# Output projection of three batches moved into the attention steps, with two rearrangements before the first step

## The chip, the cores and the metric

The kernel runs on one core of one Trainium2 chip. The time is device microseconds of one execution. The kernel before was run three times: 1149.98, 1150.86 and 1151.96 us, median 1150.86 us. One further execution was recorded by the profiler; all rows below are from that one.

## The reference, cut to what matters

```python
xn = _layernorm(x)                                   # x: (4, 2048, 256), 16 heads of 16
q, k, v = xn @ q_w, xn @ k_w, xn @ v_w               # each (4, 16, 2048, 16) after the reshape
scores = (q * sigmoid(unity_scale)) @ k.T / sqrt(16)
allowed = (j % 4 == 0) | (abs(i - j) <= 8)
attn = softmax(where(allowed, scores, -inf)) @ v
ffn  = float8_e4m3fn(clip(xn / input_scale, -448, 448)) * input_scale @ w_dq.T + bias
x + (attn @ o_w + o_b) + ffn                         # (4, 2048, 256)
```

## The kernel before, in words

The 8192 rows are 16 chunks of 512 rows (CH), four in each batch (CPB). There are two parts, one after the other on every engine.

**The projection part** (`part_project`) goes once over the 16 chunks, c = 0 to 15. For a chunk TensorE (PE) makes q (L551), the transposes of the next chunk (L561), k (L572), v (L582) and the fp8 linear product (L597, waits for `y8_ready`). ScalarE (ACT) writes the high halves of q and k as f16 (L327, L347) and copies v out of PSUM (L354); VectorE (DVE) writes the low halves (L435, L440) and adds the linear product to `base`, which holds x (L376); GpSimd (POOL) rounds to fp8 (L296, L299). SyncE (SP) stores q and k of a chunk in twelve DMAs of 128 KB (L262) and v in four of 256 KB (L256). There are two buffers for these halves, so ACT's L327 of chunk c waits until all twelve stores of chunk c-2 have landed (`qk_stored`).

**The attention part** (`part_attend`) has 64 steps: 16 groups of four heads (four groups a batch), each with four chunks of 512 queries. The steps are unrolled, and the order within a step is written out by hand in `tensor_attend.body`. A step has three strands:

- *Units.* Ten of them a step, for queries one and two steps ahead: PE makes scores with queries on partitions (L1092 far keys, L1103 and L1110 near keys), DVE reduces each to a maximum (L1002, L1005). Two units fit into PSUM. The maxima go through DVE L985, four small POOL instructions (L798 to L804), a PE transpose (`score_peaks`, L1048), an ACT copy (L927) and two DMAs by SP (`move_negmax`, L846) into rows of `q_op`, and the first scores of the next step wait for that.
- *Scores and weights.* PE makes scores with keys on partitions (L1057, L1067, L1070), ACT takes the exponential (L934, L939), PE multiplies with v (L1127, L1134). `SCORES` lists the order; the scores go round three PSUM banks, and PE may refill a bank when ACT is done with it (`s_used`).
- *The division.* ACT copies the result (L918), SP moves the sums (L838), DVE inverts them (L978), SP stores and broadcasts them (L870, L888), POOL multiplies (L789), SP stores the step's result to `attn_dram` (L892).

`Step(0, -2)` and `Step(0, -1)` hold the units and negated maxima that step 0 needs. Before them SP waits for all stores of the projection part and loads v (`load_v`, L823), and ACT waits for these stores too.

After the last step the output projection runs by itself: for each of the 16 chunks the transposed attention result is loaded (`load_heads`, L760, two DMAs of 256 KB: SP for the first batch, within the last steps, ACT for the others), PE multiplies it with `o_w` (L1207, and L1229 for the last chunk, in quarters), DVE adds it to `base` (L1018, L1029) and SP stores the chunk (L904, 512 KB; L907, 128 KB each).

## Time and profile before

| | |
|---|---|
| median of three runs | 1150.86 us |
| the profiled execution | 1153.22 us, of which the span 1151.4 us |
| busy, share of the span | PE 94%, DVE 82%, ACT 70%, POOL 22% |
| TensorE clock granted, mean | 0.976 of full speed |
| DMA, mean | 131 GB/s |
| projection part | 0 to about 237 us |
| steps 0 to 63 | 266 to 1084 us |
| output projection | 1084 to 1151 us |

"Busy" of PE is from a matmul's start to its modelled end. Matmuls overlap in the array, so a PE that is busy in the profile may still be between two starts with nothing to start; how far apart the starts are tells more. The span begins at the core's first instruction.

### The profile page before, as it was taken

The page shows a single profiled execution, that of the slowest core. Times are in us where ns is not written, and L with a number is a line of the kernel's source. Part 1 is how long each engine was busy: PE and PEld are TensorE (multiplying, and loading weights), DVE is VectorE, ACT ScalarE, POOL GpSimd, SP SyncE. Part 2 cuts the span into 40 slices and gives each one's busy share as a digit, 9 for nine tenths or more (in the row PEclk, how much of TensorE's full clock was granted, in tenths as well). Part 3 has the DMA queues.
Part 4 walks back from the last instruction along what each step waited for, and adds up shares of the span by engine and source line. Part 5 has one row for each costly group of instructions (what it writes and reads, how often), then busy time and mean ns, then how long its engine had stood idle before and what let it go on. Part 6 is the DMA issues. An engine that isn't in the chain of part 4 may idle for free.

```text
span 1151.4 us, 28768 instructions
## 1 busy us (share of the span) xinstructions
PE 1080.5 (94%) x10944; PEld 492.7 (43%) x10944; DVE 944.7 (82%) x1203; ACT 808.6 (70%) x1524; POOL 249.3 (22%) x381
## 2 busy tenths in 40 slices
PE   5899999947999999999999999999999999999896
PEld 3566666512333333333333334333333333333585
DVE  5888777475999999999999999999999999998132
ACT  2443444215888888888888888888888888888500
POOL 1433333210221222122121212212121212212100
PEclk9999999956999999999999999999999999999998
DMA  6677777662223333333333333333333333232367
GB/s 190 190 230 229 218 229 235 197 194 66 90 85 110 96 102 91 109 96 94 101 105 98 91 96 113 94 95 97 109 95 92 100 104 101 89 104 85 97 247 271
DMA packets 192506, 150.74 MB, mean 131 GB/s; under 512 B 35628, under 2 KB 171564, under 8 KB 192364
## 3 DMA queue, kind: packets, MB, share of 16 engines
q1 hardware_dynamic: 188424, 142.10, 40.4%
q10 hardware_dynamic: 3952, 6.88, 1.7%
q8 instruction: 85, 1.39, 0.5%
q14 instruction: 45, 0.37, 0.1%
HBM read 79.86 MB, written 67.77 MB: 128 GB/s over the span
## 4 chain that ended last, share of the span: by engine, by line
PE 66%; DVE 10%; SPq 8%; issue 7%; DMA 6%; ACT 1%; POOL 0%; ACTq 0%; DVEq 0%; POOLq 0%
PE ps_attend L1127 16%; PE ps_attend L1057 12%; PE ps_attend L1092 9%; DVE peak_far L1002 9%; PE ps_attend L1134 6%; SPq L262 5%; PE ps_attend L1067 4%; PE ps_attend L1103 3%; DMA heads<-attn_dram 3%; PE ps_attend L1070 3%; SPq L256 3%; PE ps_project L582 2%; PE ps_project L551 2%; PE ps_project L572 2%; PE ps_attend L1110 2%
## 5 line engine op out<-in xcount | busy, mean ns | idle before, releaser
L1002 DVE TENSOR_REDUCE peak_far<-ps_attend 128x2 f32<-128x1024 f32 x512 | 608.6, 1221 | 55.1 <-PE ps_attend L1092 51.5
L934 ACT ACTIVATE probs<-ps_attend 128x512 f32<-128x512 f32 x1024 | 539.1, 597 | 54.9 <-PE ps_attend L1057 51.8
L1127 PE MATMUL ps_attend<-probs,v_op 128*32 128x512 f32 x2048 | 273.4, 606 | 0.0
L1057 PE MATMUL ps_attend<-q_op,k_op 51*128 51x512 f16 x1024 | 259.5, 387 | 14.4 <-DMA q_op<-negmax_rows 10.7
L1092 PE MATMUL ps_attend<-k_op,q_op 48*128 48x512 f16 x1024 | 186.6, 389 | 17.1 <-DVE peak_far L1002 15.5
L1057 PEld LDWEIGHTS ps_attend<-q_op,k_op 51*128 51x128 f16 x1024 | 77.8, 93 | 209.3 <-ACT probs L934 135.6
L939 ACT ACTIVATE probs<-ps_attend 108x512 f32<-108x512 f32 x256 | 138.9, 594 | 37.3 <-PE ps_attend L1070 37.3
L798 POOL CAST negmax<-peak 128x16 bf16<-128x16 f32 x64 | 12.6, 197 | 638.0 <-DVE peak L985 638.0
L1005 DVE TENSOR_REDUCE peak_near<-ps_attend 128x8 f32<-128x864 f32 x128 | 131.0, 1023 | 11.3 <-PE ps_attend L1110 11.1
L789 POOL TENSOR_TENSOR out_rows<-out_rows,share_rows 128x512 f32<-128x512 f32 x64 | 81.3, 1270 | 48.6 <-DMA share_rows<-shares_dram 46.0
L1067 PEld LDWEIGHTS ps_attend<-mask_q,mask_k 48*108 48x108 bf16 x1024 | 59.9, 125 | 67.8 <-ACT probs L934 55.3
L1092 PEld LDWEIGHTS ps_attend<-k_op,q_op 48*128 48x128 f16 x1024 | 49.9, 94 | 88.7 <-DVE peak_far L1002 70.0
L1067 PE MATMUL ps_attend<-mask_q,mask_k 48*108 48x128 bf16 x1024 | 78.6, 227 | 0.8 <-ACT probs L934 0.8
L327 ACT ACTIVATE qk_parts<-ps_project,ranges 128x1024 f16<-128x1024 f32 x16 | 17.8, 1114 | 82.2 <-DMA k_dram<-qk_parts 38.4
L1070 PE MATMUL ps_attend<-q_op,k_op 51*108 51x128 f16 x1024 | 73.6, 217 | 0.0
L1134 PE MATMUL ps_attend<-probs,v_op 108*32 108x128 f32 x2048 | 69.2, 276 | 0.0
L1127 PEld LDWEIGHTS ps_attend<-probs,v_op 128*32 128x32 f32 x2048 | 40.4, 108 | 58.4 <-issue 58.3
L296 POOL TENSOR_TENSOR quant<-quant,power 128x1024 f32<-128x1024 f32 x16 | 37.7, 2356 | 119.5 <-DVE qk_parts L440 84.8
L1103 PE MATMUL ps_attend<-mask_k,mask_q 48*128 48x216 bf16 x512 | 58.9, 259 | 3.3 <-DVE peak_far L1002 1.6
L551 PE MATMUL ps_project<-xnT,wq 128*128 128x512 f32 x128 | 60.3, 616 | 1.2 <-ACT xnT L334 1.2
L1070 PEld LDWEIGHTS ps_attend<-q_op,k_op 51*108 51x108 f16 x1024 | 61.5, 126 | 0.0
L1134 PEld LDWEIGHTS ps_attend<-probs,v_op 108*32 108x32 f32 x2048 | 52.1, 109 | 15.7 <-issue 13.7
(80 smaller groups left out, 1043.2 us busy)
## 6 DMA issues: line engine op xcount, KB each, us to landing
v_dram<-v_sb SPq DMA_DIRECT2D x64, 256.0 KB, 4.1
share_rows<-shares_dram SPq DMA_DIRECT2D x64, 256.0 KB
attn_dram<-out_rows SPq DMA_DIRECT2D x64, 256.0 KB, 5.7
v_op<-v_dram SPq DMA_DIRECT2D x48, 288.0 KB
q_dram<-qk_parts SPq DMA_DIRECT2D x96, 128.0 KB
k_dram<-qk_parts SPq DMA_DIRECT2D x96, 128.0 KB
q_op<-q_dram SPq DMA_DIRECT2D x128, 96.0 KB, 2.4
k_op<-k_dram SPq DMA_DIRECT2D x64, 144.0 KB, 3.1
```

The source lines that it names most:

```text
L551: last = nc.tensor.matmul(ps_q[:, m], wq[:, i, m * P:(m + 1) * P], xnT[:, k, i], start=(i == 0), stop=(i == KC - 1))
L934: ins = nc.scalar.activation(probs[:, r, h], ps_s[st.bank(kind)], ACT.Exp, scale=undo)
L939: ins = nc.scalar.activation(probs[0:WIN, ROUNDS - 1, h], ps_s[st.bank(kind)][0:WIN], ACT.Exp, scale=undo)
L1002: ins = nc.vector.tensor_reduce(peak_far[:, :, p, tile], banks, AX_X, ALU.max)
L1005: ins = nc.vector.tensor_reduce(peak_near[:, :, tile:tile + 2].rearrange("q f t p -> q f (t p)"), banks[:, :, 0:2 * PAIRS * WIN].rearrange ...
L1057: nc.tensor.matmul(bank, k[half(f, KM), keys], q[half(f, KM), p], start=True, stop=True).then_inc(s_ready, 1)
L1067: nc.tensor.matmul(banks[f][0:WIN, cols], mask_k[half(f), at_mask:at_mask + WIN], mask_q[half(f), tile * P:(tile + 1) * P], start=True, st ...
L1070: ins = nc.tensor.matmul(banks[f][0:WIN, cols], k[half(f, KM), at:at + WIN], q[half(f, KM), p, cols], start=False, stop=True)
L1092: nc.tensor.matmul(banks[f], q[half(f), p, tile * P:(tile + 1) * P], k[half(f), strided(p):strided(p) + NS], start=True, stop=True).then_i ...
L1103: nc.tensor.matmul(banks[f][:, whole].rearrange("q (p w) -> q p w", p=PAIRS), mask_q[half(f), st.queries(d) * CH + tile * P:st.queries(d) ...
L1127: ins = nc.tensor.matmul(ps_o[h * VW:(h + 1) * VW], v[:, r, h * VW:(h + 1) * VW], probs[:, r, h], start=(r == 0), stop=False)
L1134: ins = nc.tensor.matmul(ps_o[h * VW:(h + 1) * VW, t * P:(t + 1) * P], v[0:WIN, tile, h * VW:(h + 1) * VW], probs[0:WIN, r, h, t * P:(t + ...
```

## The change

Three things are changed; the arithmetic stays the same.

1. *Projection part.* The four v stores of a chunk are issued by ACT behind its own copy of v, and no longer by SP. The linear product of the last chunk (`linear(15)`) and the addition of it (`add_linear(15)`) leave the projection part: PE and DVE do them between `Step(0, -2)` and `Step(0, -1)`.
2. *Before the first step.* The steps -2 and -1 now come ahead of the waits for the stores on SP and ACT, and so ahead of `load_v(0, 0)`.
3. *Output projection.* A new kind of entry, `("out",)`, stands in `SCORES` behind `("negmax",)`. It is there in the steps 17, 19, ... 63, 24 of them, and does half a chunk of the batches 0 to 2: PE makes two tiles of 128 rows into one of the three score banks (`score_out`), ACT copies the bank to `y_rows`, POOL adds that to `base`. SP loads the chunk in the step before (`fetch_heads`, in every fourth step from 16 on) and stores it in the step after its second half. Only the four chunks of the last batch stay behind the steps.

```diff
@@ sync_project
-                for w, part in ((0, HI), (0, LO), (1, HI), (None, None), (1, LO)):
-                    if w is None:
-                        sp.wait_ge(v_copied, c + 1)
-                        for t in range(TT):
-                            sp.dma_start(dram["v"]..., v_sb[:, k, t]...).then_inc(v_stored[k], 16)
-                        continue
+                for w, part in ((0, HI), (0, LO), (1, HI), (1, LO)):
@@ scalar_project, behind the copy of v
+                    act.wait_ge(v_copied, c + 1)
+                    for t in range(TT):
+                        act.dma_start(dram["v"]..., v_sb[:, k, t]...).then_inc(v_stored[k], 16)
@@ SCORES
-    ("near", 0), ("far", 2, 0), ("negmax",), ("far", 3, 1), ("far", 3, 0),
+    ("near", 0), ("far", 2, 0), ("negmax",), ("out",), ("far", 3, 1), ("far", 3, 0),
+OUT_FIRST, OUT_EVERY = G * CPB + 1, 2
@@ gpsimd_attend, end of a step
+            if out_part(st.n) is not None:
+                part = out_part(st.n)
+                rows = base[:, part // 2, part % 2 * CH:(part % 2 + 1) * CH]
+                pool.wait_ge(bias_added, part // 2 + 1)
+                pool.wait_ge(s_used, st.entry(("out",)))
+                nc.gpsimd.tensor_tensor(rows, rows, y_rows[:, part % 2], ALU.add).then_inc(part_added, 1)
@@ sync_attend
+        def fetch_heads(b, n):
+            for k in range(OUTS):
+                sp.wait_ge(attn_stored[k], 16 * len(range(k, ((b + 1) * G - 1) * CPB + n + 1, OUTS)))
+            for i in range(KC):
+                load_heads(sp, b, n, i)
@@ sync_attend, end of a step
+            if st.n >= G * CPB and (st.n % CPB == 0 or st.n >= STEPS):
+                b, n = (st.n // (G * CPB) - 1, st.n // CPB % CPB) if st.n < STEPS else (B - 1, st.n - STEPS)
+                fetch_heads(b, n)
+            if out_part(st.n - 1) is not None and out_part(st.n - 1) % 2 == 1:
+                part = out_part(st.n - 1)
+                sp.wait_ge(part_added, part + 1)
+                sp.dma_start(out_tiles[part // 2], totals[:, part // 2]).then_inc(out_stored, 16)
@@ scalar_attend
+                elif kind[0] == "out":
+                    part = out_part(st.n)
+                    if part >= 2:
+                        act.wait_ge(part_added, part - 1)
+                    ins = nc.scalar.activation(y_rows[:, part % 2], ps_s[st.bank(kind)], ACT.Copy)
@@ tensor_attend
+        def score_out(st):
+            part = out_part(st.n)
+            n = part // 2 % CPB
+            bank = free_score(st, ("out",))
+            pe.wait_ge(heads_loaded[n], 16 * KC * (part // 2 // CPB + 1))
+            for t in range(2):
+                tile = 2 * (part % 2) + t
+                for i in range(KC):
+                    ins = nc.tensor.matmul(bank[:, t * H:(t + 1) * H], heads[:, n, i, tile * P:(tile + 1) * P],
+                                           keep["wo"][:, i], start=(i == 0), stop=(i == KC - 1))
+            ins.then_inc(s_ready, 1)
@@ tensor_attend; in vector_attend the same with add_last_linear
-        unrolled(body)
-        for n in range(CPB):
-            project(0, n)
-        with pe.Fori(1, B - 1) as j:
-            for n in range(CPB):
-                project(j, n)
+        body(Step(0, FIRST))
+        done["last_linear"]()
+        for n in range(FIRST + 1, LAST + 1):
+            body(Step(0, n))
```

On SP, in the middle of the projection part, the rows of one chunk were these before:

```order
L262 DMA q_dram<-qk_parts 8x16x512 [waits hi_ready]
L262 DMA q_dram<-qk_parts 8x16x512 x3
L262 DMA q_dram<-qk_parts 8x16x512 [waits lo_ready]
L262 DMA q_dram<-qk_parts 8x16x512
L262 DMA k_dram<-qk_parts 8x16x512 [waits hi_ready]
L262 DMA k_dram<-qk_parts 8x16x512 x3
L256 DMA v_dram<-v_sb 128x4x128 [waits v_copied]
L256 DMA v_dram<-v_sb 128x4x128 x3
L262 DMA k_dram<-qk_parts 8x16x512 [waits lo_ready]
L262 DMA k_dram<-qk_parts 8x16x512
```

And these are the last chunk and what follows it on SP now (L255 is the store of q and k, L865 `move_negmax`, L850 `load_v`):

```order
L255 DMA q_dram<-qk_parts 8x16x512 [waits hi_ready]
L255 DMA q_dram<-qk_parts 8x16x512 x3
L255 DMA q_dram<-qk_parts 8x16x512 [waits lo_ready]
L255 DMA q_dram<-qk_parts 8x16x512
L255 DMA k_dram<-qk_parts 8x16x512 [waits hi_ready]
L255 DMA k_dram<-qk_parts 8x16x512 x3
L255 DMA k_dram<-qk_parts 8x16x512 [waits lo_ready]
L255 DMA k_dram<-qk_parts 8x16x512
L865 DMA q_op<-negmax_rows 3x8x128 [waits s_used,pads_stored]
L865 DMA q_op<-negmax_rows 3x8x128
L850 DMA v_op<-v_dram 128x4x128 [waits v_stored0,qk_stored0,qk_stored1,v_copied,v_stored1,lo_ready,base_ready]
L850 DMA v_op<-v_dram 36x16x128 x3
```

The v stores have left SP, and the two DMAs of the negated maxima stand ahead of the loads of v, where before they stood behind them.

On PE, in a step with an output part (step 17), the rows from the first weighing on are now (L1169 was L1127, L1076 was L1048, L1099 was L1057, L1134 was L1092):

```order
L1169 MATMUL ps_attend<-probs,v_op 32x512 [waits s_used,out_copied]
L1169 MATMUL ps_attend<-probs,v_op 32x512 x3
L1076 MATMUL ps_attend<-ident_bf,negmax 128x128 [waits negmax_ready,s_used]
L1089 MATMUL ps_attend<-wo,heads 128x256 [waits heads_loaded0,s_used]
L1089 MATMUL ps_attend<-wo,heads 128x256 x3
L1099 MATMUL ps_attend<-q_op,k_op 128x512 [waits s_used] x2
L1134 MATMUL ps_attend<-k_op,q_op 128x512 [waits u_used]
L1134 MATMUL ps_attend<-k_op,q_op 128x512
```

The two rows of L1089 are new; the rest is as it was. At the end of SP's program, from the last sums on, there is now (L898 shares stored, L910 shares broadcast, L914 result stored, L780 heads loaded, L927 and L943 a chunk of the output stored):

```order
L857 DMA sums<-out_rows 64x1x32 [waits shares_ready,out_copied]
L780 DMA heads<-attn_dram 128x1x512 [waits attn_stored2,attn_stored1,attn_stored0]
L780 DMA heads<-attn_dram 128x1x512
L927 DMA out<-base 128x4x256 [waits part_added]
L898 DMA shares_dram<-shares 64x32 [waits shares_loaded,shares_ready,s_ready]
L910 DMA share_rows<-shares_dram 128x1x512 [waits shares_stored,attn_ready]
L914 DMA attn_dram<-out_rows 128x512
L780 DMA heads<-attn_dram 128x1x512 [waits attn_stored2,attn_stored1,attn_stored0]
L780 DMA heads<-attn_dram 128x1x512
L914 DMA attn_dram<-out_rows 128x512 [waits attn_ready,s_ready]
L780 DMA heads<-attn_dram 128x1x512 [waits attn_stored2,attn_stored1,attn_stored0]
L780 DMA heads<-attn_dram 128x1x512
```

The last shares now stand behind the load of one chunk and the store of another, and the loads of the last chunks wait for the results that have just been stored.

## Rows read from the trace of the kernel before

**Rows 1.** Busy time by stage (stretch, its length, engines, clock, DMA share, GB/s).

```profile
150.00:220.00 70.00, 69.23 (x304) 44.62 (x303) 49.58 (x113) 28.08 (x35) 25.71 (x11) 1.00 0.71 221
220.00:250.00 30.00, 17.81 (x87) 9.12 (x85) 15.43 (x16) 3.19 (x4) 2.56 (x2) 0.73 0.67 203
...
500.00:700.00 200.00, 196.65 (x2432) 75.49 (x2424) 185.95 (x191) 176.40 (x348) 42.71 (x84) 1.00 0.33 99
```

**Rows 2.** Timeline from the last chunk to step 0 (start, us, what, idle before).

```profile
217.56 3.60 PE L551 MATMUL ps_project<-xnT,wq 128*128 128x512 f32 x8
...
220.71 3.75 SPq L256 DMA_DIRECT2D v_dram<-v_sb  x4
...
224.43 3.62 PE L582 MATMUL ps_project<-wv,xnT 128*128 128x256 f32 x16
...
230.48 1.11 ACT L327 ACTIVATE qk_parts<-ps_project,ranges 128x1024 f16<-128x1024 f32 x1 [13.44 <-DMA k_dram<-qk_parts]
...
234.14 3.29 PE L597 MATMUL ps_project<-w_parts,y 128*128 128x256 f16 x16 [6.09 <-POOL y L299]
...
237.36 0.61 PE L1092 MATMUL ps_attend<-k_op,q_op 48*128 48x512 f16 x4
...
237.47 1.28 DVE L376 SCALAR_TENSOR_TENSOR base<-ps_project,scales,base 128x1024 f32<-128x1024 f32 x1 [2.91 <-PE ps_project L597]
...
238.67 3.48 DVE L1002 TENSOR_REDUCE peak_far<-ps_attend 128x2 f32<-128x1024 f32 x3
...
249.88 0.18 DVE L985 TENSOR_TENSOR peak<-peak_far,peak_near 128x16 f32<-128x16 f32 x1
...
251.41 0.27 PE L1048 MATMUL ps_attend<-ident_bf,negmax 128*128 128x128 bf16 x1 [0.90 <-POOL negmax L804]
...
256.67 0.27 ACT L927 ACTIVATE negmax_rows<-ps_attend 48x128 f16<-48x128 f32 x1 [23.01 <-DMA k_dram<-qk_parts]
...
259.59 1.95 SPq L846 DMA_DIRECT2D q_op<-negmax_rows  x2
...
265.90 1.03 PE L1057 MATMUL ps_attend<-q_op,k_op 51*128 51x512 f16 x3 [10.57 <-DMA q_op<-negmax_rows]
```

**Rows 3.** Timeline of the middle of a step (same columns).

```profile
700.31 1.09 ACT L934 ACTIVATE probs<-ps_attend 128x512 f32<-128x512 f32 x2
...
707.07 0.77 PE L1057 MATMUL ps_attend<-q_op,k_op 51*128 51x512 f16 x2
...
708.93 0.39 PE L1057 MATMUL ps_attend<-q_op,k_op 51*128 51x512 f16 x2
...
709.33 1.52 SPq L846 DMA_DIRECT2D q_op<-negmax_rows  x2
...
709.67 1.23 DVE L1002 TENSOR_REDUCE peak_far<-ps_attend 128x2 f32<-128x1024 f32 x1 [0.16 <-PE ps_attend L1092]
...
712.02 1.09 ACT L939 ACTIVATE probs<-ps_attend 108x512 f32<-108x512 f32 x2 [0.57 <-PE ps_attend L1070]
...
712.99 1.09 ACT L934 ACTIVATE probs<-ps_attend 128x512 f32<-128x512 f32 x2
```

**Rows 4.** Timeline of the output projection (same columns).

```profile
1083.65 0.59 SPq L838 DMA_DIRECT2D sums<-out_rows  x1
...
1097.97 1.23 DVE L1018 TENSOR_TENSOR base<-ps_attend,base 128x1024 f32 x1 [2.23 <-PE ps_attend L1207]
...
1139.00 3.72 PE L1229 MATMUL ps_attend<-wo,heads 128*128 128x256 f32 x16 [0.25 <-DMA heads<-attn_dram]
...
1142.76 0.42 DVE L1029 TENSOR_TENSOR base<-ps_attend,base 128x256 f32<-128x256 f32 x1 [0.44 <-PE ps_attend L1229]
```

**Rows 5.** DMA issues (what, queue, count, KB each, median us to landing).

```profile
attn_dram<-out_rows SPq DMA_DIRECT2D x64, 256.0 KB, 5.7
...
shares_dram<-shares SPq DMA_DIRECT2D x64, 8.0 KB, 1.7
...
out<-base SPq DMA_DIRECT2D x4, 128.0 KB, 3.7
```

More of the change, by code:

```diff
@@ L585, in body @@
                     last.then_inc(v_ready, 1)
[L587 to L589 removed]
                     if ahead:
[L591 to L601 removed]
+                        linear(c, k)
             chunks(pe, body)
@@ L639, in entries, with out_part @@
 def entries(s):
-    return [kind for kind in SCORES
-            if (-1 <= s and s + 1 < STEPS if kind == ("negmax",) else 0 <= s < STEPS)]
+    there = {("negmax",): -1 <= s and s + 1 < STEPS, ("out",): out_part(s) is not None}
+    return [kind for kind in SCORES if there.get(kind, 0 <= s < STEPS)]
+def out_part(s):
+    if not (OUT_FIRST <= s < STEPS and (s - OUT_FIRST) % OUT_EVERY == 0):
+        return None
+    return (s - OUT_FIRST) // OUT_EVERY
 def part_attend(nc, io, dram, keep, out, ctx, done):
```

165 lines of the change are left out of this document (79 added, 86 removed).

## The prediction

> **What bounds the kernel now.** I read the busy time by stage first, then the timeline at the two seams (projection part to step 0, step 63 to the end), then the timeline of one step. In the middle of the projection part PE is busy 69.23 us of 70 at full clock; in the steps 196.65 of 200, with DVE at 186 and ACT at 176 [rows 1]. Between the two lies a hole: from 220 to 250 us PE is busy 17.81 of 30, at a mean clock of 0.73 [rows 1]. PE has finished the last v at 228.05 (224.43 + 3.62), and the first score of step 0 starts at 265.90 [rows 2]. The second soft place is the end: from the last sums at 1083.65 to the end of the span at 1151.4 are 67.75 us. There PE projects 16 chunks, and a chunk costs it 3.46 us when they follow one another (DVE's add of 1.23 us and its 2.23 us of waiting for PE) [rows 4]. That is 55.4 us of 67.75, so the end is mostly PE work too, and the DMA chain of the last step (sums, shares, result) hides beneath it.
>
> The whole change is therefore an exchange of three terms: the hole gets shorter, the steps get longer, the end gets shorter.
>
> **Term 1, the hole.** Why does ACT's L327 of chunk 15 come at 230.48, when q of that chunk was ready at 221.16 (217.56 + 3.60)? It waited for a k store of chunk 13 [rows 2]. SP is late: it issues twelve stores at about 0.65 to 0.95 us and four v stores in 3.75 us [rows 2], and with the loads of k and q for step 0 this is more than the 12.9 us that PE needs for a chunk (56 of the 304 matmul records of 70 us [rows 1]). Without the v stores SP has some 3.7 us to spare per chunk, and it had three chunks to catch up. So L327 goes at about 221.2, and L299, L347 and L435 behind it are through before the last v matmul ends. PE then starts its units at about 228.1, right behind v.
> The ten reductions took DVE from 238.67 to 249.88, 11.2 us [rows 2]. Now they start at 228.6; between the fifth and the sixth stand the add of the biases (0.4 us), the wait for 16 linear matmuls (3.29 us at the low clock, half of that at the high one) and their add, 1.28 us [rows 2]: together 3 us. Peak at 242.8. The POOL chain and the transpose take 1.5 us as before (249.88 to 251.41), and then ACT copies at once, at 244.6, where before it sat 23 us until the stores had landed, and SP loaded v (in 3 us) ahead of L846 [rows 2]. In a step 3.0 us pass at most from the issue of L846 to the first score (709.33 to 712.35, when ACT's pair at 712.99 has been fed) [rows 3]; before step 0 it was 6.3 us with the v loads in front. Step 0 starts at about 247.9 instead of 265.90: **minus 18 us**. The stores must have landed by then, since ACT still waits for them before the first exponential. The last can be issued when k's low half is there, about 227.5; ACT's own v stores go out from 229.1 to 233, and with 4 to 6 us to landing they are in by 239, 9 us early. The price on ACT: 3.75 us of issuing per chunk, at the end of a chunk, where by its busy time of 28 us in 70 [rows 1] it has room; it must be through when q of the next chunk is ready, some 4.2 us after the copy of v (16 linear and 8 q records of PE, 1.7 + 3.6, less 1.0 for the copy). If it isn't, y8 is late, and y8 is used 8 us after q. I take 17.5 for the term; ends 9 (only L327's lateness goes) and 21.
> The DMA engines are busy 0.71 of the time in the projection part and 0.67 after it [rows 1], not full, while SP's queue issues without a gap. The Trainium skill, "DMA: Bandwidth & Descriptors", section "Issuing engines are not separate DMA queues", says that DMAs of all engines share the same 16 engines and that issuing from several saves only the time to initiate them, usually small. By that rule the v stores' move should bring next to nothing; here the time to initiate is what SP has run out of. It is a rival below.
>
> **Term 2, the steps.** A part is eight fp32 matmuls of 128x256 in two records each, half a chunk: 3.46 / 2 = 1.73 us of PE [rows 4]. PE is busy 98% of the steps, which leaves 0.2 us a step; but busy overstates. Two L1057 take 0.39 us when nothing holds them (708.93) and 0.77 at 707.07, where the second waits for a bank [rows 3]. There are eight such places in a step, of 0.1 to 0.5 us each by the starts against the shortest spacing of the same pair, about 2 us of 12.68 (700.31 to 712.99 [rows 3]) in which PE has nothing to start. So a part costs between nothing and 1.73 plus ACT's copy of 0.6. Which waits could it fill? Only those whose cause runs on while PE does the part. At the place where the part stands, DVE has just emptied its queue (it waits 0.16 us for PE's next unit, at 709.67) and ACT has too: it does the tiny L927 there, and idles 0.57 us before 712.02 [rows 3]. Neither has work in hand; both stand still for most of the 1.73 us, and the waits of PE behind that place come back as they were. DVE's head start saves PE about 0.3 us (the wait before the near unit goes), and ACT's copy, 0.5 us in its queue, fills the gap of 0.57 but delays the two pairs behind it, which returns as 0.4 us of PE waiting in the next step's first pair. I take 1.95 us for a part, **24 x 1.95 = plus 47 us**; ends 0 and 2.3 x 24 = 56. POOL's add (1.27 us on an engine that is busy 22%) and SP's three more DMAs in every fourth step come behind the negated maxima, 12 us before the next; they are covered by that slack, and the shares that then queue behind 1 MB are 4 us later where POOL has 10 us in hand. I cost them nothing; if the cover fails it is at most 1 us in each of 12 steps.
>
> **Term 3, the end.** Twelve chunks leave it. What is late next is the DMA chain of step 63, now uncovered. From T, the issue of the last sums: they queue behind the shares and the result of the step before, T+4.8 (a store of 256 KB lands in 5.7 us [rows 5]). Inversion, then the shares' store, in SP's queue behind the load of one chunk and the store of another, 1 MB at the end stage's rate: T+9.5 (unqueued it would be 1.7 us [rows 5], T+7.3). Broadcast, 256 KB as well, estimated at 5.3: T+14.8. POOL 1.3: T+16.1. Store 5.7: T+21.8. Two loads of the last chunk, 0.65 us of issue and 5 to landing by the same row: T+27.4. PE 3.72 [rows 4]: T+31.1. The last add and store: from DVE's last start (1142.76) to the end it is 8.6 us before, with stores queued in front; a landing of 3.7 [rows 5] and the issue make about 5.5. T+36.7, plus 1 for the clock: PE idles for 3 to 8 us between chunks, and at 228 such a gap was followed by the low clock (the 3.29 us of L597 [rows 2]). A whole chunk at half speed would be 3.7 us more. **67.75 - 37.7 = minus 30 us**; ends 26 and 34.
>
> **Sum.** -17.5 + 47 - 30 = -0.5 us. The profiled execution took 1153.22 us, 2.4 above the median of 1150.86; I apply the difference to the median: 1150.4.
>
> **Rivals.**
> *The part fills PE's waits.* PE has 2 us of them a step. If half the part vanished in them (1.0 us a part): 24 us, sum -23.5, 1127. For it: the waits exist. Against it: both partners are empty at that place.
> *ACT's copy becomes the bound (slower).* ACT is at 88% in the steps, its 20 exponentials close on each other in fours, and the copy stands in front of four of them. If PE's next pairs wait for it in full, a part costs 1.73 + 0.57 = 2.3 us, 55 us in all, sum +7.7: 1158.5. It decides from 2.0 us a part on (that is 47.5 us, what the seams give back); slower by more than 0.2% from 2.1. Against it: the gap of 0.57 us [rows 3].
> *The transfers bound the seam.* If 203 to 221 GB/s [rows 1] is all the DMA engines give, the stores end no earlier than about 253, and step 0 starts at 254, gain 12 instead of 17.5: sum +5, 1156. This is what the rule of the skill would give. Against it: the share of 0.67.
> *The seams give more.* Chunk 15 and step 0 at the high clock, and the shares not held by the queue: -20 and -34, sum -7: 1144.
>
> **How the numbers follow.** No change can be told from one below 0.2%, 2.3 us. My forecast 0.55 (own range 1145 to 1155: faster 0.15, within 0.34, slower 0.06); filled waits 0.1, faster; ACT's copy 0.15, slower but for 0.02; transfers 0.1, slower 0.08 and within 0.02; more from the seams 0.1, faster 0.1. Together faster 0.35, within 0.38, slower 0.27. The range takes in all but the filled waits and half of the slow rival: 1139 to 1158.
>
> **What the profile after should show.** Step 0's first score near 248. Steps with a part 14.5 us and the ones behind them 12.8. PE never waits for the loads of heads within the steps. From the last sums to the end 38 us, with PE idle between the four chunks. The forecast is wrong if L327 of chunk 15 still waits, if a step with a part is under 14 or over 15 us, or if the end is outside 34 to 42.

## The result, and the profile after

| | before | after |
|---|---|---|
| median of four runs, same chip | 1151.07 us | 1171.05 us |
| all runs | 1149.98 to 1151.96 | 1169.97 to 1176.72 |
| span of the profiled execution | 1151.4 us | 1169.7 us |
| ratio after / before | | 1.0183 [1.0159, 1.0208] |

The change makes the kernel 1.8% slower. 1150.4 us had been forecast, with a range of 1139 to 1158, which does not hold the result.

The spans can be cut at the same two events as in the prediction, the first score before step 0 and the issue of the last sums:

| | before | after | difference | predicted |
|---|---|---|---|---|
| start to the first score (Term 1) | 265.90 | 265.25 | -0.65 | -17.5 |
| first score to the last sums (Term 2) | 817.75 | 870.14 | +52.4 | +47 |
| last sums to the end (Term 3) | 67.75 | 34.3 | -33.4 | -30 |
| span | 1151.4 | 1169.7 | +18.3 | -0.5 |

Terms 2 and 3 are wrong by 5.4 and 3.4 us, in opposite directions. Term 1 is missing as a whole, 17 us of it, and the rest of this text is mostly about that.

Busy time by stage after the change (columns as in [rows 1]):

```profile
150.00:220.00 70.00, 68.08 (x286) 43.61 (x285) 50.29 (x124) 26.86 (x36) 23.61 (x11) 0.96 0.75 221
220.00:250.00 30.00, 23.92 (x95) 13.54 (x94) 13.08 (x15) 8.52 (x10) 7.05 (x3) 0.84 0.71 198
500.00:700.00 200.00, 195.04 (x2302) 79.61 (x2294) 172.87 (x177) 167.47 (x330) 46.14 (x85) 1.00 0.36 109
```

Compare 150 to 220 us with [rows 1]: the matmul records fall from 304 to 286, and the transferred bytes stand still at 221 GB/s, although two queues carry them now. Over the middle of the projection part as a whole (60 to 205 us; the same view, first of the kernel before, then of the kernel after) the rate falls, and PE is idle 6.6 us where before it was idle 0.8:

```profile
60.00:205.00 145.00, 144.23 (x631) 93.60 (x629) 111.14 (x276) 60.59 (x78) 51.83 (x22) 1.00 0.73 230
```

```profile
60.00:205.00 145.00, 138.40 (x589) 88.73 (x587) 104.14 (x254) 54.93 (x71) 49.43 (x21) 0.98 0.74 218
```

The projection part has slowed down. These are rows of the timeline of one such delay in the kernel after (L247 loads a chunk of x, L255 stores q and k, L354 stores v, L546 is the addition that was L376, L584 the transposes that were L561):

```profile
128.22 4.17 ACTq L354 DMA_DIRECT2D v_dram<-v_sb  x4
...
130.30 1.59 SPq L247 DMA_DIRECT2D base<-in_x  x1
...
138.39 1.41 DVE L379 BATCH_NORM_STATS2 stats<-base 128x6 f32 x4 [6.95 <-DMA base<-in_x]
...
147.57 1.28 DVE L546 SCALAR_TENSOR_TENSOR base<-ps_project,scales,base 128x1024 f32 x1
...
148.99 1.94 PE L584 MATMUL ps_project<-ident,xn 128*128 128x128 f32 x8 [3.96 <-DVE base L546]
```

The load of x goes into SP's queue at 130.30, when three of ACT's four v stores are out already. It takes 1.59 us to issue and lands 8.0 us after its start; in the kernel before, the loads from 60 to 205 us take 0.41 to 0.63 us to issue and land after 4.3 to 5.5. DVE's statistics at 138.39 waited 6.95 us for it, all that DVE has behind them is late, and PE stands still 3.96 us for L546. PE's first q matmuls of successive chunks are 12.9 us apart in the kernel before but for one 13.9, measured from chunk 3 on. After, three of these gaps are 15.8, 20.0 and 16.8 us. So q of the last chunk starts at 229.92, where it was 217.56 [rows 2].

From there on (same view):

```profile
229.92 3.60 PE L574 MATMUL ps_project<-xnT,wq 128*128 128x512 f32 x8
...
240.65 1.12 ACT L320 ACTIVATE qk_parts<-ps_project,ranges 128x1024 f16<-128x1024 f32 x1 [11.24 <-DMA k_dram<-qk_parts]
...
251.83 3.92 SPq L255 DMA_DIRECT2D q_dram<-qk_parts  x6
...
255.80 4.59 SPq L255 DMA_DIRECT2D k_dram<-qk_parts  x6
...
261.85 0.27 ACT L966 ACTIVATE negmax_rows<-ps_attend 48x128 f16<-48x128 f32 x1 [18.02 <-PE ps_attend L1076]
262.20 1.60 SPq L865 DMA_DIRECT2D q_op<-negmax_rows  x2
...
265.25 1.06 PE L1099 MATMUL ps_attend<-q_op,k_op 51*128 51x512 f16 x3
265.98 1.28 ACT L978 ACT_TABLE_LOAD   x1 [3.86 <-PE ps_attend L1099]
267.27 4.25 ACT L978 ACTIVATE probs<-ps_attend 128x512 f32<-128x512 f32 x8
```

L320 (L327 before) still waits for a k store of two chunks ago, 11.24 us. The seam itself is shorter: from q of chunk 15 to the first score it is 35.3 us, where it was 48.3. The projection part ahead of it is 12.4 us longer, and takes that back. A new detail stands at the end: the table for the exponential (1.28 us) is loaded only after the first score is there.

The steps with a part, one of the slow kind (L927 stores a chunk of 512 KB, L898 and L910 the shares, L1089 the part, L973 ACT's copy of it):

```profile
647.44 1.34 SPq L780 DMA_DIRECT2D heads<-attn_dram  x2
648.82 0.46 SPq L927 DMA_DIRECT2D out<-base  x1
649.40 0.54 SPq L898 DMA_DIRECT2D shares_dram<-shares  x1
...
655.66 0.60 SPq L910 DMA_DIRECT2D share_rows<-shares_dram  x1
...
656.89 0.62 SPq L857 DMA_DIRECT2D sums<-out_rows  x1
...
657.91 1.95 PE L1089 MATMUL ps_attend<-wo,heads 128*128 128x256 f32 x8
...
659.90 0.60 ACT L973 ACTIVATE y_rows<-ps_attend 128x512 f32<-128x512 f32 x1 [1.51 <-PE ps_attend L1089]
...
662.64 0.34 DVE L1010 RECIPROCAL shares<-sums 64x32 f32<-64x32 f32 x1 [0.88 <-DMA sums<-out_rows]
```

A part takes PE 1.95 us. From ACT's copy of the negated maxima in one step to that in the next, a plain step is 12.68 us (before and after, one step in sixteen is 0.27 longer) and a step with a part 14.63. But of the 23 that can be measured so (the last one has no next), ten are 14.76 to 15.44: the shares' 8 KB, behind a load and a store of 512 KB each in SP's queue, are awaited until 655.66, 6 us after their issue (1.7 in the median, [rows 5]), so the next sums are issued late and DVE waits for them.

The end (L1248 was L1207, L1269 was L1229):

```profile
1135.39 0.54 SPq L857 DMA_DIRECT2D sums<-out_rows  x1
...
1140.45 0.35 DVE L1010 RECIPROCAL shares<-sums 64x32 f32<-64x32 f32 x1 [14.12 <-DMA sums<-out_rows]
...
1144.22 5.61 PE L1248 MATMUL ps_attend<-wo,heads 128*128 128x256 f32 x16 [10.27 <-DMA heads<-attn_dram]
1145.59 0.54 SPq L910 DMA_DIRECT2D share_rows<-shares_dram  x1
...
1151.41 1.26 POOL L809 TENSOR_TENSOR out_rows<-out_rows,share_rows 128x512 f32<-128x512 f32 x1 [10.34 <-DMA share_rows<-shares_dram]
...
1163.40 3.62 PE L1269 MATMUL ps_attend<-wo,heads 128*128 128x256 f32 x16
```

Behind the steps PE is idle between chunks, as predicted, and the chain of DMAs is bare. With T the issue of the last sums, as in the prediction, the inversion comes at T+5.1 (4.8 predicted), broadcast at T+10.2 (9.5), POOL at T+16.0 (14.8), the last chunk at T+28.0 (27.4), the end at T+34.3 (37.7).

### The profile page after: what moved, and what is told of

Same layout as the page of the kernel before. It is cut to its first block, busy times and chain, and to the rows that moved or that the text cites. A ratio compares the mean times of both kernels' runs of the same rounds, so it can differ in the third digit from the quotient of the medians.

```text
span 1169.7 us, 28716 instructions
## 1 busy us (share of the span) xinstructions
PE 1089.5 (93%) x10944; PEld 495.3 (42%) x10944; DVE 930.1 (80%) x1191; ACT 820.8 (70%) x1548; POOL 279.7 (24%) x405
## 4 chain that ended last, share of the span: by engine, by line
PE 51%; SPq 14%; DMA 14%; DVE 11%; issue 8%; ACT 1%; ACTq 0%; DVEq 0%
PE ps_attend L1169 14%; SPq L255 11%; PE ps_attend L1099 10%; DVE peak_far L1034 8%; PE ps_attend L1134 8%; DMA shares_dram<-shares 6%; DMA sums<-out_rows 5%; PE ps_attend L1176 5%; PE ps_attend L1109 3%; PE ps_attend L1112 2%; PE ps_attend L1089 2%; PE ps_attend L1145 2%; PE ps_attend L1152 2%; ACT probs L978 1%; PE ps_attend L1248 1%
## 5 line engine op out<-in xcount | busy, mean ns | idle before, releaser
L1169 PE MATMUL ps_attend<-probs,v_op 128*32 128x512 f32 x2048 | 273.4, 606 | 0.0
L1099 PE MATMUL ps_attend<-q_op,k_op 51*128 51x512 f16 x1024 | 264.7, 386 | 6.6 <-ACT probs L978 2.8
L1134 PE MATMUL ps_attend<-k_op,q_op 48*128 48x512 f16 x1024 | 186.3, 389 | 26.7 <-DVE peak_far L1034 14.0
L1099 PEld LDWEIGHTS ps_attend<-q_op,k_op 51*128 51x128 f16 x1024 | 77.5, 93 | 212.4 <-ACT probs L978 144.9
L1134 PEld LDWEIGHTS ps_attend<-k_op,q_op 48*128 48x128 f16 x1024 | 49.8, 94 | 97.3 <-DVE peak_far L1034 69.7
L1109 PEld LDWEIGHTS ps_attend<-mask_q,mask_k 48*108 48x108 bf16 x1024 | 59.9, 125 | 67.8 <-ACT probs L978 55.3
L320 ACT ACTIVATE qk_parts<-ps_project,ranges 128x1024 f16<-128x1024 f32 x16 | 17.8, 1115 | 89.3 <-DMA k_dram<-qk_parts 41.9
L289 POOL TENSOR_TENSOR quant<-quant,power 128x1024 f32<-128x1024 f32 x16 | 37.7, 2355 | 126.7 <-DVE qk_parts L434 88.2
L1169 PEld LDWEIGHTS ps_attend<-probs,v_op 128*32 128x32 f32 x2048 | 40.4, 108 | 59.5 <-issue 56.4
L595 PE MATMUL ps_project<-xnT,wk 128*128 128x512 f32 x128 | 61.3, 624 | 0.0
```

The costliest lines, as they stand in the source:

```text
L1099: nc.tensor.matmul(bank, k[half(f, KM), keys], q[half(f, KM), p], start=True, stop=True).then_inc(s_ready, 1)
L1109: nc.tensor.matmul(banks[f][0:WIN, cols], mask_k[half(f), at_mask:at_mask + WIN], mask_q[half(f), tile * P:(tile + 1) * P], start=True, st ...
L1134: nc.tensor.matmul(banks[f], q[half(f), p, tile * P:(tile + 1) * P], k[half(f), strided(p):strided(p) + NS], start=True, stop=True).then_i ...
L1169: ins = nc.tensor.matmul(ps_o[h * VW:(h + 1) * VW], v[:, r, h * VW:(h + 1) * VW], probs[:, r, h], start=(r == 0), stop=False)
```

## The experiments

All are cut at the same places for comparison: c15 is the start of PE's q of chunk 15, step 0 is the first exponential, T here the end of the last step's copy of the result on ACT (0.02 to 0.8 us before the issue of the last sums). Times are of the profiled execution; the ratio is that of the timed runs to those of the kernel before on the same chip.

| kernel | c15 | step 0 | step 0 to T | T to end | ratio |
|---|---|---|---|---|---|
| before | 217.6 | 266.5 | 817.1 | 67.8 | 1 |
| after | 229.9 | 267.3 | 867.3 | 35.1 | 1.0183 [1.0159, 1.0208] |
| v_act | 232.8 | 270.9 | 817.3 | 66.3 | 1.0017 [0.9989, 1.0045] |
| seam | 219.2 | 260.2 | 817.1 | 65.5 | 0.9942 [0.9921, 0.9963] |
| parts | 220.7 | 268.5 | 869.3 | 35.8 | 1.0172 [1.0145, 1.0199] |
| after_vsp | 220.2 | 260.7 | 868.2 | 35.2 | 1.0107 [1.0080, 1.0134] |
| seam_vact | 228.6 | 268.6 | 816.6 | 66.8 | 1.0005 [0.9989, 1.0021] |
| act_tiny | 219.2 | 266.3 | 816.6 | 67.1 | 1.0019 [1.0008, 1.0031] |
| spread | 218.4 | 259.0 | 864.1 | 33.9 | 1.0056 [1.0040, 1.0073] |
| pos | 217.4 | 259.1 | 867.5 | 33.9 | 1.0064 [1.0042, 1.0086] |
| halfk | 219.2 | 260.7 | 843.7 | 32.5 | 0.9890 [0.9862, 0.9918] |
| seam_table | 217.7 | 257.0 | 817.9 | 65.1 | 0.9919 [0.9903, 0.9935] |
| seam_v15 | 218.5 | 257.4 | 817.5 | 67.5 | 0.9924 [0.9904, 0.9944] |
| seam_v15_k | 221.6 | 253.2 | 817.5 | 65.5 | 0.9850 [0.9832, 0.9869] |

### The three parts of the change, each alone

*v_act*: the kernel before, with only the v stores moved.

```diff
@@ sync_project
-                for w, part in ((0, HI), (0, LO), (1, HI), (None, None), (1, LO)):
-                    ... (four v stores)
+                for w, part in ((0, HI), (0, LO), (1, HI), (1, LO)):
@@ scalar_project, behind the copy of v
+                    act.wait_ge(v_copied, c + 1)
+                    for t in range(TT):
+                        act.dma_start(dram["v"]..., v_sb[:, k, t]...).then_inc(v_stored[k], 16)
```

> The kernel before, with one edit: the four v stores of a chunk are issued by ACT. Theory T (the transfers are the limit: a store issued by SP takes longer to issue when ACT issues beside it, so nothing is saved, and x loads and q/k stores land later and hold PE): PE stalls in the projection part as in the changed kernel (three gaps of 3 to 7 us), step 0 starts 9 to 13 us later than before, time about 1162 us. Theory I, my prediction's (SP's time to issue was the limit): step 0 about 9 us earlier, 1142 us. Theory A (the time to issue on ACT, 4 us a chunk, delays ACT's own halves of q and k): also slower, but then ACT's L320 comes late because ACT was busy, not because a store had not landed.

Measured: 1155.56 us, against 1152.95 before, ratio 1.0017 [0.9989, 1.0045]: no difference clear of noise, and neither of the times that were expected (1162 and 1142). Its ten runs scatter from 1148.89 to 1162.95. In the profile chunk 15 starts 15.3 us later than before and step 0 is 38.0 us behind it, where it was 49.0: the delay of the projection part stands here without the rest of the change, and most of it (11 of 15 us) is taken back in the hole, where PE had waited anyway.

*seam*: the steps -2 and -1 ahead of the waits, `linear(15)` between them, v stores left on SP.

```diff
@@ sync_attend
-        sp.wait_ge(...)  (all stores)
-        load_v(0, 0)
-        unrolled(body)
+        for n in range(FIRST, 0):
+            body(Step(0, n))
+        sp.wait_ge(...)  (all stores)
+        load_v(0, 0)
+        for n in range(0, LAST + 1):
+            body(Step(0, n))
@@ the same on ACT; on PE and DVE
+        body(Step(0, FIRST))
+        done["last_linear"]()
+        for n in range(FIRST + 1, LAST + 1):
+            body(Step(0, n))
```

> The kernel before, with the seam alone: steps -2 and -1 ahead of the waits for the stores, last linear product between them; v stores stay on SP, the output projection stays behind the steps. Negated maxima are then issued right behind SP's last store (253.6 us before) instead of behind the landing and the loads of v (259.6), and without the v loads in front they land in 3 us: step 0 at 257 instead of 265.9, time about 1142 us (faster by 9). If the gain needs the v stores on ACT, it is under 3 us.

Measured: 1145.62 us, ratio 0.9942 [0.9921, 0.9963], step 0 6.3 us earlier (8.9 were expected). In the timeline of SP, the last stores and what follows (L850 moves the negated maxima):

```profile
249.10 3.92 SPq L256 DMA_DIRECT2D v_dram<-v_sb  x4
253.07 1.82 SPq L262 DMA_DIRECT2D k_dram<-qk_parts  x2
254.99 1.59 SPq L850 DMA_DIRECT2D q_op<-negmax_rows  x2
```

ACT's copy of the negated maxima was ready at 252.2 (251.89 + 0.27), and its DMA stands in SP's queue behind the stores of chunk 15 until 254.99. The rearrangement pays, and what limits it is SP's backlog of stores.

*parts*: the output parts alone, the rest as before (the diff of `SCORES`, `score_out`, `fetch_heads` and POOL's addition shown above).

> The kernel before, with the output parts in the steps alone (v stores on SP, waits and last linear product as before). Read from the changed kernel's trace the steps lengthen by 50.2 us and the end shortens by 32.7: 1168.5 us, slower by 17.5. If instead the parts are paid for by what the seam left behind (late loads), less than 10 us slower.

Measured: 1173.79 us, ratio 1.0172 [1.0145, 1.0199]; the steps are 52.2 us longer (50.2 expected), the end is 32.0 us shorter (32.7).

*after_vsp*: the whole change, with the v stores back on SP.

> The changed kernel, with one edit: the v stores are issued by SP again. Theory T: the stalls of PE in the projection part go, the seam's gain shows: step 0 at 257, 10 us earlier than in the changed kernel, time about 1161 us. Theory I: step 0 later than in the changed kernel, over 1175 us.

Measured: 1165.37 us, ratio 1.0107 [1.0080, 1.0134], chunk 15 at 220.2 and step 0 at 260.7. Taking the v stores back makes the span 5.6 us shorter than that of after; step 0 is 6.6 us earlier (10 expected), and the steps are 0.9 longer. The parts alone are within 0.2% of the whole change: the seam's gain and the v stores' loss cancel in it.

### What the v stores on ACT cost

*seam_vact*: seam, with the v stores on ACT as in v_act. *act_tiny*: the kernel before, and ACT issues four more DMAs of 8 KB a chunk where it would issue v's; the v stores stay on SP.

```diff
@@ scalar_project, behind the copy of v
+                    act.wait_ge(v_copied, c + 1)
+                    for t in range(TT):
+                        act.dma_start(dram["tiny"][k * TT + t], v_sb[:, k, t, 0, 0:D]).then_inc(v_stored[k], 16)
```

> The seam alone, with the v stores issued by ACT: what the changed kernel has without its output parts. Theory T (the transfers are the limit): SP's q and k stores take about 1.0 us to issue instead of 0.66, PE stalls in the projection part, step 0 about 5 us later than in the seam (260.2): 1150.5 us. Theory I: over 5 us earlier than the seam, under 1141 us.

> The kernel before, with four more DMAs of 8 KB by ACT behind each copy of v; SP still issues the v stores. It gives ACT the work of issuing without moving any bytes off SP. Theory A (ACT's issuing time delays PE): stalls as in v_act. Theory T: none, since 32 KB a chunk beside 3 MB is nothing; the gaps between the chunks' first matmuls stay 12.9 us and the time is within 2 us of before.

Measured: seam_vact 1152.76 us, ratio 1.0005 [0.9989, 1.0021], where seam had 0.9942; its chunk 15 starts at 228.6, 9.4 us later than seam's. act_tiny 1154.03 us, ratio 1.0019 [1.0008, 1.0031], with chunk 15 at 219.2 and step 0 where it was; its longest gap between chunks is 14.4 us. Four DMAs of 8 KB hold ACT's queue for 1.9 to 2.3 us, so act_tiny gives ACT about half of the 4.2 us of the real stores. It costs some 2 us (0.9 to 3.6 by the interval). ACT was not what held up the chunk shown above either: it was through with its v stores at 132.39 and then waited for a k store until 135.73. What delays the chunks comes with the 256 KB stores themselves in a second queue. SP's issue times say how. In the middle of the projection part (60 to 205 us), mean us of one DMA:

| | q on SP | k on SP | v |
|---|---|---|---|
| before | 0.63 | 0.69 | 0.69, SP |
| act_tiny | 0.64 | 0.71 | 0.67, SP |
| after | 1.12 | 0.90 | 1.00, ACT |
| v_act | 1.12 | 0.87 | 1.02, ACT |
| seam_vact | 1.15 | 0.86 | 0.97, ACT |

A q or k store takes 0.66 us to issue alone and 1.0 beside ACT's. SP had twelve of these and four v stores a chunk, 10.7 us by the row of before (6 x 0.63 + 6 x 0.69 + 4 x 0.69); with four fewer it has 12.1 (6 x 1.12 + 6 x 0.90), more than with them. Some 0.15 us between one DMA and the next and the load of x come on top, and in none of these five kernels does SP's queue stand longer than 0.8 us at a time. Landing shows it too (DMA issues of after, then of before: queue, count, KB, median us):

```profile
v_dram<-v_sb ACTq DMA_DIRECT2D x64, 256.0 KB, 6.3
```

```profile
v_dram<-v_sb SPq DMA_DIRECT2D x64, 256.0 KB, 4.1
```

The loads of x tell which stores did the harm. The three kernels with all v stores on ACT (after, v_act, seam_vact) have 30 such loads between 60 and 205 us. Eight were issued when two or more of ACT's v stores of a chunk had just gone out; they landed after 7.6 to 8.8 us. The other 22 landed after 4.6 to 6.4. And these kernels have eight gaps of more than 15 us between the q of successive chunks from chunk 3 on: each follows one of these eight loads. In act_tiny, with up to four pieces of 8 KB ahead of the load, it lands after 4.5 to 5.9.

What an issue consists of is less clear. In the kernel before no q or k store takes SP less than 0.60 us, half of them take up to 0.62, and five of the eight loads of k for step 0 in seam_v15 (below), 48 and 144 KB, take 0.60 as well: alone, a store's time is nearly a fixed price. In the kernel after, the 18 q and k stores of the same stretch that meet no v store on its way take 0.62 in the mean, the 99 that meet one 1.07. So the second queue's stores stretch the issue of the first one's and delay the load of x, on which everything depends. What they compete for was not separated: a DMA of 8 KB in act_tiny has fewer bytes than a v store, and fewer pieces too. The DMA engines as such were not at their limit; in the output projection of the kernel before they moved more (view as in [rows 1]):

```profile
1105.00:1115.00 10.00, 9.67 (x45) 8.54 (x46) 3.55 (x3) 0.00 (x0) 0.79 (x1) 1.00 0.93 335
```

### What the parts cost in the steps

*spread*: after_vsp, with the store of a finished chunk two steps later, so that it does not stand in the step that also loads one. *halfk*: spread, but each part multiplies only the first half of the 256 inputs, so half of the projection of batches 0 to 2 is left out of the output. *pos*: spread, with the part earlier in the step, where PE waits while work is in hand, and the heads loaded a step earlier.

```diff
@@ spread: sync_attend, end of a step
-            if out_part(st.n - 1) is not None and out_part(st.n - 1) % 2 == 1:
-                part = out_part(st.n - 1)
+            if out_part(st.n - 3) is not None and out_part(st.n - 3) % 2 == 1:
+                part = out_part(st.n - 3)
@@ halfk: score_out
-                for i in range(KC):
-                    ins = nc.tensor.matmul(..., heads[:, n, i, ...], keep["wo"][:, i], start=(i == 0), stop=(i == KC - 1))
+                ins = nc.tensor.matmul(..., heads[:, n, 0, ...], keep["wo"][:, 0], start=True, stop=True)
@@ pos: SCORES
-    ("far", 0, 0), ("far", 0, 1), ("far", 2, 1), ("far", 1, 0), ("far", 1, 1),
-    ("near", 0), ("far", 2, 0), ("negmax",), ("out",), ("far", 3, 1), ("far", 3, 0),
+    ("far", 0, 0), ("far", 0, 1), ("out",), ("far", 2, 1), ("far", 1, 0), ("far", 1, 1),
+    ("near", 0), ("far", 2, 0), ("negmax",), ("far", 3, 1), ("far", 3, 0),
```

> The changed kernel with v stores on SP, and the stores of the output two steps later, so that SP no longer issues a store of 512 KB right behind a load of 512 KB (step 20, 24, ...). In the changed kernel the shares' store then took 6 us to land instead of 1.7, the sums came late and DVE stood 0.9 us in 11 of the 24 steps with a part (15.0 to 15.5 us instead of 14.63). If the queue behind 1 MB is the cause, all these steps fall to 14.63: 4 to 5 us less than after_vsp (1165.4), about 1161. If the load alone is enough, no change.

> As spread, but each part leaves out one of the two halves of the sum (four matmuls instead of eight), so the output is not the reference's. If the part's price is PE's time, a step with a part falls from 14.63 by 0.86 us to 13.77; if ACT's copy or the bank sets it, by less.

> As spread, with the output part at another place of the step: behind the second unit, ahead of the unit for far keys of tile 0, where PE waits 0.32 us for DVE in the trace of before, and with the heads loaded one step earlier. My account of the steps says that a part costs its 1.73 us of PE and ACT's copy, less the waits that run on while PE does it. There DVE has two units in hand: the part then costs about 1.4 us instead of 1.95, 24 x 0.55 = 13 us less than spread: about 1148. If a part costs the same everywhere (PE is simply full), no change.

Measured for spread: 1158.83 us, ratio 1.0056 [1.0040, 1.0073]. Of the 23 steps with a part 20 are 14.63 us now, and three are 14.90, those that are 0.27 longer before as well. From step 0 to T it is 864.1, which is 817.1 + 24 x 1.95 = 863.9. The shares still land 4.5 to 5.9 us after their issue where they stand behind a load of 512 KB alone, and no step pays for that; behind the load and the store it was about 6, and ten steps did. The rows of ACT give one such step, from 567.92 to 582.56:

```profile
567.92 0.27 ACT L967 ACTIVATE negmax_rows<-ps_attend 48x128 f16<-48x128 f32 x1 [0.18 <-PE ps_attend L1077]
569.71 0.60 ACT L974 ACTIVATE y_rows<-ps_attend 128x512 f32<-128x512 f32 x1 [1.51 <-PE ps_attend L1090]
...
582.56 0.27 ACT L967 ACTIVATE negmax_rows<-ps_attend 48x128 f16<-48x128 f32 x1 [0.18 <-PE ps_attend L1077]
```

In halfk the part is 1.08 us for 1.95, and the step is shorter by the same 0.87, here from 566.98 to 580.75:

```profile
566.98 0.27 ACT L967 ACTIVATE negmax_rows<-ps_attend 48x128 f16<-48x128 f32 x1 [0.18 <-PE ps_attend L1077]
567.90 0.60 ACT L974 ACTIVATE y_rows<-ps_attend 128x512 f32<-128x512 f32 x1 [0.65 <-PE ps_attend L1089]
...
580.75 0.27 ACT L967 ACTIVATE negmax_rows<-ps_attend 48x128 f16<-48x128 f32 x1 [0.18 <-PE ps_attend L1077]
```

It measured 1139.73 us, ratio 0.9890 [0.9862, 0.9918], in two runs. The price of a part is PE's time for it, one to one; nothing of it vanishes in PE's waits at that place, and ACT's copy adds nothing of its own (it is the same 0.60 us in both). The two lengths also say why a part is 1.95 us and not the 1.73 of the prediction. A part is four matmuls, in eight records of the profile (the prediction and the expectation of halfk call them eight matmuls). Halving them saves 0.87 us, so all eight records make 1.74, and 0.21 stands once per part, however much it multiplies.

pos puts the part into waits with work in hand. Thirteen of the 23 steps with a part are 14.29 us there, so at this place a part costs 1.61 us: 0.34 us of it fills waits. The other ten are 14.65 to 17.53 us; plain steps stay at 12.68. The sum to T is 867.5, 3.4 worse than spread; 1160.06 us, ratio 1.0064 [1.0042, 1.0086], where 1148 was expected. In each of these ten steps DVE waits 0.6 to 1.9 us for the sums. One of them (L899 stores the shares, L911 broadcasts them, L858 moves the next sums, L1012 inverts them):

```profile
574.03 1.32 SPq L781 DMA_DIRECT2D heads<-attn_dram  x2
575.45 0.51 SPq L899 DMA_DIRECT2D shares_dram<-shares  x1
...
581.11 0.60 SPq L911 DMA_DIRECT2D share_rows<-shares_dram  x1
...
582.58 0.60 SPq L858 DMA_DIRECT2D sums<-out_rows  x1
...
588.12 0.34 DVE L1012 RECIPROCAL shares<-sums 64x32 f32<-64x32 f32 x1 [1.50 <-DMA sums<-out_rows]
...
589.44 0.39 PE L1136 MATMUL ps_attend<-k_op,q_op 48*128 48x512 f16 x2 [1.50 <-DVE peak_near L1039]
590.08 1.08 ACT L980 ACTIVATE probs<-ps_attend 128x512 f32<-128x512 f32 x2 [1.24 <-PE ps_attend L1101]
```

It is the delay of the kernel after again: the shares stand behind a load of heads, their broadcast and the next sums go out late, DVE waits for the sums, PE 1.50 us for DVE, and ACT 1.24 for PE. In spread the shares are as late behind a load and nothing waits for them; here, with part and load in other steps, ten steps do. Whether the new place would keep its gain with the load where it was has not been run. At 1.61 us in all 24, an estimate from these rows, the steps would be 38.6 us longer, still more than the 32 to 34 us that the end gives back. No arrangement tried brought a part below what the end gives back.

### Towards a better kernel

*seam_table*: seam, and one exponential of a single column on ACT behind its copy of the negated maxima, so that the table is loaded while ACT waits. *seam_v15*: seam_table, and the v stores of the last chunk alone on ACT. *seam_v15_k*: seam_v15, and the eight loads of k for step 0 (144 and 48 KB) issued by ACT, half in chunk 12 and half in chunk 13, where SP issued all in chunk 12.

```diff
@@ seam_table: scalar_attend, ahead of the waits
+                nc.scalar.activation(keep["warm"][:], keep["undo"][:], ACT.Exp)
@@ seam_v15: sync_project
+                    if w is None and isinstance(c, int) and c == B * CPB - 1:
+                        continue
@@ seam_v15: scalar_project
+                    if isinstance(c, int) and c == B * CPB - 1:
+                        ... (four v stores as in v_act)
@@ seam_v15_k: sync_project
-                    load_k(sp, dram, keep["k_op"][0], keep["k_loaded"][0], 0)
@@ seam_v15_k: scalar_project
+                    if isinstance(c, int) and B * CPB - CPB <= c < B * CPB - CPB + 2:
+                        f = c - (B * CPB - CPB)
+                        ...
+                        load_k(act, dram, keep["k_op"][0], keep["k_loaded"][0], 0, [(f, 0), (f, 1)])
```

> The seam alone, with one instruction more: ACT takes the exponential of one column ahead of its wait for the stores. In the seam's profile the load of the table for Exp (1.28 us) stood between the first scores (258.9) and the first exponential (260.2); before the change it lay in the wait for the negated maxima. If that load is on the path, step 0's first exponential comes 1.3 us earlier and the time is 1.3 us under the seam's (1145.6): about 1144, ratio to before about 0.993. If the stores' landing is what holds ACT there, no change.

> The seam with the early table load, and the v stores of the last chunk alone issued by ACT; in the chunks before, SP issues them. Nothing is left in the projection part that a slower SP could hold up. If the stores' landing is what ends the seam and SP's queue is late by its own time to issue, these four (3.9 us) leave the queue ahead of the last k stores: step 0 up to 3 us earlier, 1140 us. By theory T (bytes are the limit) under 1 us, and the last q and k stores take over 0.8 us each to issue.

> As seam_v15, and the eight loads of k for step 0 (48 and 144 KB each, 0.6 us to issue, 7 us of SP's queue in chunk 12) are issued by ACT behind its copies of v in the chunks 12 and 13. These are small, so here the time to issue should count more than the bytes: SP is 5 to 7 us less late, L327 of chunk 15 comes before 227 instead of 230.7, step 0 about 4 us earlier, 1137 us. By theory T in its strict form again nothing, or a stall of PE in chunk 13 or 14.

Measured: seam_table 1142.50 us, ratio 0.9919 [0.9903, 0.9935]. Rows of ACT, first of seam, then of seam_table:

```profile
258.89 1.28 ACT L948 ACT_TABLE_LOAD   x1 [6.73 <-PE ps_attend L1076]
260.19 2.06 ACT L948 ACTIVATE probs<-ps_attend 128x512 f32<-128x512 f32 x4
```

```profile
250.12 1.28 ACT L965 ACT_TABLE_LOAD   x1
...
256.96 4.25 ACT L948 ACTIVATE probs<-ps_attend 128x512 f32<-128x512 f32 x8 [5.35 <-PE ps_attend L1077]
```

The table's load has gone into a wait. Step 0 is 3.2 us earlier; 1.5 us of that is chunk 15, which started earlier in this execution, so the table accounts for 1.3 and some 0.4 is left. The intervals of seam and seam_table overlap, so the timed runs alone do not show the table's gain. seam_v15 measured 1144.22 us, 0.9924 [0.9904, 0.9944], no different from seam_table (up to 3 us were hoped for): ACT issues its four stores from 232.85 to 237.69, and L329 (L327) had waited 11.63 us for a k store all the same. seam_v15_k is the fastest of all: 1135.78 us, ratio 0.9850 [0.9832, 0.9869]. Rows of ACT from chunk 15 on:

```profile
225.27 1.11 ACT L328 ACTIVATE qk_parts<-ps_project,ranges 128x1024 f16<-128x1024 f32 x1 [4.16 <-PE ps_project L590]
...
249.00 0.27 ACT L956 ACTIVATE negmax_rows<-ps_attend 48x128 f16<-48x128 f32 x1 [15.83 <-PE ps_attend L1083]
...
253.16 4.25 ACT L963 ACTIVATE probs<-ps_attend 128x512 f32<-128x512 f32 x8 [2.37 <-PE ps_attend L1092]
```

L328 no longer waits for a store; it waits for PE, as Term 1 had promised for the whole change. In seam_v15 the eight loads took SP from 206.69 to 212.54, 5.9 us out of the 12.9 of a chunk, when SP was late already. With them gone, L328 comes at 225.27 where L329 came at 229.64, and step 0 at 253.2. The move has its price: chunk 14 takes 16.8 us instead of 12.9, and PE starts chunk 15 3.1 us later, which may be part of why L328 finds its stores landed. The expectation had named such a stall. ACT issued the first four loads from 195.97 to 199.29, and its copy of q came only then (L328 at 199.40, where seam_v15 has it at 196.87). Whether the other queue or the spreading over two chunks brought the gain was not separated.

## Why the prediction was wrong, point by point

**Term 1, the hole: -17.5 predicted, -0.65 measured. The step that failed** is "Without the v stores SP has some 3.7 us to spare per chunk". It took the 0.65 to 0.95 us that a store occupies SP's queue for a price of its own, which stays when ACT issues beside SP. Alone that is nearly so (0.60 to 0.62 us for half of the q and k stores), but not beside v stores in ACT's queue: these make SP's q and k stores 1.5 times as long, and SP ends up with 12.1 us a chunk for twelve stores instead of 10.7 for sixteen. The load of x, of which the prediction does not speak, then lands after up to 8.0 us instead of 5, and chunk 15 starts 12.4 us late. v_act and seam_vact show both without the rest of the change, and act_tiny shows that small DMAs from ACT do neither.
The prediction weighed the rule of the Trainium skill, "DMA: Bandwidth & Descriptors", section "Issuing engines are not separate DMA queues" (all issuers share the same engines, so spreading saves only the time to initiate). It set the rule aside for the DMA share of 0.67 and a queue "without a gap". The trace agrees with the rule: 230 GB/s with one queue, 218 with two, at a share of 0.73 and 0.74 (60 to 205 us). A share below 1 and a queue without a gap did not mean that a second queue would add anything. The rival *the transfers bound the seam* had 0.1 and 1156 us; it named the competition and saw only half of it, since it charged the stores before step 0 and not the projection part ahead.
That L327 of chunk 15 would come right behind q was the named sign; it waited 11.24 us. What follows it was sized well: 3.4 us from ACT's copy of the negated maxima to the first score (3.3 predicted). The table's 1.28 us was not in the sum; in the kernel before the two events are 0.6 us apart, after 2.0.

**Term 2, the steps: +47 predicted, 50 to 52 measured.** The 1.95 us for a part is what the profile shows (14.63 - 12.68), but the way to it was partly luck. A part is 1.95 us of PE, not 1.73, and the step pays just that. The prediction's own terms, 1.73 less 0.3 for DVE's head start and 0.4 more for ACT's copy, make 1.83 and not the 1.95 that it took. Neither of the two small terms shows as such; halfk leaves no room for a cost beside PE's time. "Waits with no work in hand don't fill" held; pos found 0.34 us a part in waits with work in hand, and lost it to late sums. The cost that the prediction set at nothing, the shares behind 1 MB in SP's queue, was 3 to 4 us in all (868.2 in after_vsp against 864.1 in spread), inside its bound of 1 us in 12 steps. The plain steps are 12.68 (12.8 predicted); ten of the steps with a part are above 14.7, six of them beyond the 15 us that the prediction named as a sign of being wrong.

**Term 3, the end: -30 predicted, -33.4 measured,** with each link of the chain of DMAs within 1.3 us. What was over-priced is the last link, from the last chunk's start to the end (6.3 us for 10.3), because that chunk ran at full clock (3.62 us, where 1 us was added for the clock) and 2.7 us were left for its last add and store, priced 5.5; the last store landed 1.8 us after its issue, where 3.7 was taken.

**The exchange as such.** It could have been seen without the hole. Behind the steps a chunk costs 3.46 us [rows 4]; taking twelve away frees 41.5 us, of which the bare chain of step 63 eats 8, so a chunk gives back 33.4 / 12 = 2.8 us. In the steps it costs 2 x 1.95 = 3.9. The prediction had both numbers (47 and 30) and balanced the 17 us between them with Term 1. With Term 1 gone the kernel is slower by just these.

## What to carry to other kernels

A queue that issues without a gap and DMA engines that are busy 0.7 of the time do not tell that a second queue will help. Here moving the bulk stores to it bought nothing, and let them go ahead of the loads on which the pipeline depends. Look at what each DMA of the first queue takes to issue, and each load to land, after the move: if both grow, the stores compete. Moving small loads out of a bad place did pay, with a smaller price of the same kind. Test such a move alone, since a second gain in the same change hides its loss. Before work is moved from an exposed end into a full loop, compare its price per piece in both places, less what the piece was covering at the end.

## What the runs showed of the hardware that was not expected

- A q or k store of 128 KB occupies SP's queue 0.66 us in the mean alone, never under 0.60, and 1.0 us while ACT's queue stores 256 KB pieces, up to 2.7 us for one. With 8 KB pieces in ACT's queue it stays at 0.67.
- A load of x of 512 KB that is issued right behind two or more such pieces of the other queue lands after 7.6 to 8.8 us, otherwise after 4.6 to 6.4 (30 loads in three kernels).
- Eight KB behind 1 MB in the same queue were awaited 6 us after their issue, against a median of 1.7; behind 512 KB in spread, 4.5 to 5.9.
- A part of eight matmul records costs PE 1.95 us and one of four 1.08: 0.22 us for each record and 0.21 once.
- At the end of the kernel after, PE works in pieces with idle time between. PE has nothing to do from 1133.95 to 1144.22. At 1137.8, within that gap, the granted clock falls to half, and it is back at 1148.1, within the chunk that follows (L1248), which takes 5.61 us; the last chunk, at full clock, takes 3.62.
- The kernels with all v stores on ACT scatter more: v_act 14 us between its lowest and highest of ten runs, seam_vact 8.4 of twelve, the kernel before 8.7 of thirteen and 5.1 of twenty-three on the same chips.
